# A two-layer attention and expert kernel: rotation of the keys one tile earlier, the maxima's scores ahead of the mix, and the routing product over 112 rows

## What is computed

```python
kv_r = kv_c * cos + rotate_half(kv_c) * sin
scores = q_r . k_r                      # per head, 56 tokens x 1500 rows
attn = softmax(scores)
ctx_c = attn . kv_r
out = merged value and output weights applied to ctx_c
# layer 0, after the attention
cw = weights of the 4 chosen of 16 experts, 0 for the others
moe = sum over e of cw[e] * down_e(silu(gate_e x) * (up_e x))  + shared expert
```

## Time and profile before

| what | value |
|---|---|
| median of 3 runs | 3447.54 us (3446.84 to 3452.19) |
| profiled execution, own time | 3445.47 us |
| its span, first to last instruction | 3443.7 us |
| mean granted TensorE clock | 0.918 of full speed |
| PE busy | 2980.6 us, 87% |
| DVE busy | 2033.7 us, 59% |
| POOL busy | 1769.7 us, 51% |
| ACT busy | 1261.3 us, 37% |
| DMA queues | 26.6% of 16 engines' span |

### The profile page before, as it was taken

How to read it: one execution, slowest core, us unless ns; L and a number is a source line. 1 busy time by engine, 2 the same in 40 slices (tenths; PEclk the granted TensorE clock), 3 DMA queues, 4 the chain that set the end, 5 groups by cost and what they waited for, 6 DMA issues and landing times. The chain is left out here.

```text
span 3443.7 us, 43529 instructions
## 1 busy us (share of the span) xinstructions
PE 2980.6 (87%) x16008; PEld 1691.6 (49%) x16008; DVE 2033.7 (59%) x2351; ACT 1261.3 (37%) x1747; POOL 1769.7 (51%) x1008
## 2 busy tenths in 40 slices
PE   7688978899888989888897789986997699888987
PEld 6444446444464444654445544453445444454445
DVE  3576656766467664676655556455645566446645
ACT  3124434244341444333443334332442244323432
POOL 0466723676436775366672247523771177315750
PEclk9789989899988999898998889988998899988998
DMA  7423213233114231132321233203321322122310
GB/s 253 118 61 87 62 40 92 72 81 81 34 60 110 63 84 50 61 101 57 74 58 50 88 77 76 74 6 86 78 52 51 86 60 67 53 61 67 83 56 6
DMA packets 117806, 247.54 MB, mean 72 GB/s; under 512 B 30415, under 2 KB 82879, under 8 KB 110038
## 3 DMA queue, kind: packets, MB, share of 16 engines
q1 hardware_dynamic: 117590, 244.57, 26.6%
HBM read 171.24 MB, written 48.27 MB: 64 GB/s over the span
## 5 line engine op out<-in xcount | busy, mean ns | idle before, releaser
L1215 POOL TENSOR_TENSOR sums<-sums,prob 125x896 f32<-125x896 f32 x528 | 1119.8, 2121 | 174.8 <-ACT prob L1102 125.0
L1331 DVE TENSOR_REDUCE maxpart<-pair 112x2 f32<-112x1000 f32 x720 | 861.5, 1197 | 464.1 <-PE pair L851 464.1
L1102 ACT ACTIVATE prob<-wide 125x896 f32<-125x896 f32 x768 | 704.3, 917 | 886.5 <-PE wide L877 884.5
L892 PE MATMUL single<-prob,kv 125*64 125x448 f32 x3072 | 758.1, 572 | 0.9
L872 PE MATMUL wide<-qhigh,kparts 64*125 64x448 f32 x3072 | 461.6, 378 | 0.0
L851 PE MATMUL pair<-kparts,qhigh 64*112 64x500 f32 x1440 | 358.3, 494 | 61.5 <-DVE maxpart L1331 47.3
L851 PEld LDWEIGHTS pair<-kparts,qhigh 64*112 64x112 f32 x1440 | 129.3, 176 | 489.8 <-DVE maxpart L1331 399.8
L1215 POOL TENSOR_TENSOR sums<-prob 125x896 f32<-125x896 f32 x64 | 134.4, 2100 | 408.4 <-ACT prob L1102 408.4
L872 PEld LDWEIGHTS wide<-qhigh,kparts 64*125 64x125 f32 x3072 | 283.3, 187 | 110.3 <-issue 81.2
L877 PE MATMUL wide<-shift,ones_row 64*125 64x448 f32 x1536 | 290.2, 373 | 48.8 <-DMA shift<-maxrow 48.8
L872 PE MATMUL wide<-qlow,kparts 64*125 64x448 f32 x1536 | 288.3, 370 | 0.0
(11 more groups left out here) (322 smaller groups left out, 4268.9 us busy)
## 6 DMA issues: line engine op xcount, KB each, us to landing
kparts<-keys_merged SPq DMA_DIRECT2D x64, 750.0 KB, 9.0
wexp_low_values<-in_experts SPq DMA_DIRECT2D x68, 384.0 KB, 3.1
kparts<-kparts SPq DMA_DIRECT2D x96, 250.0 KB, 3.1
keys_merged<-kparts SPq DMA_DIRECT2D x32, 750.0 KB, 7.6
recip<-zrec_merged SPq DMA_DIRECT2D x112, 112.0 KB, 2.8
raw<-in_ctx SPq DMA_DIRECT2D x33, 375.0 KB
w_low_values<-w_merged SPq DMA_DIRECT2D x64, 192.0 KB, 3.1
values_merged<-kv SPq DMA_DIRECT2D x32, 375.0 KB
```

What stands on the lines that cost most here:

```text
L892: mm = pe.matmul(mix_acc[64 * half:64 * half + DC, 0:HQ], kv[:, j % 3, t, :], prob[:, (j * LT + t) % NPROB, half * HQ:(half + 1) * HQ], st ...
L1102: nc.scalar.activation(prob[:, n_ % NPROB, :].rearrange("p (a b) -> p a b", a=2), acc[0:LP, :, 0:HQ], ACT.Exp)\
L1215: nc.gpsimd.tensor_tensor(dst, first_in, prob[:, n_ % NPROB, :], ALU.add).then_inc(s["pool_sum"], 1)
L1331: V.tensor_reduce(maxpart[:, j % 2, t:NMAX:4, b], acc[0:TQ, :, 0:LB], AX.X, ALU.max).then_inc(*R.signal_drained(kind, *key))
```

## The change

- A new constant `CWLOW = 96` takes the place of 32 for the low part of `cwT` and of `pick`. Both are then 112 rows high, with zeros in partitions 16 to 95, and the product `weight` goes over 112 rows.
- `rotate(j + 3)` stands at the start of the last tile of batch j, where `rotate(j + 2)` stood at the start of tile 0; only `rotate(2)` is at tile 0 of batch 0.
- `ropecos` is at tiles 0 and 1, `rope` at tiles 2 and 3.
- `stash` is at the last tile, was at tile 9.
- `maximum(*ahead)`, which adds `smax`, is put right after `score` (and `maxneg`), ahead of `mix`, in both layers.

```diff
-            if layer == 0 and t == 0 and j + 2 < BG:
-                add("rotate", j + 2)
+            if layer == 0 and t == 0 and j == 0:
+                add("rotate", 2)
+            if layer == 0 and t == LT - 1 and j + 3 < BG:
+                add("rotate", j + 3)
...
             add("score", j, t, region=t % 2)
             if j + 1 < BG and t == 8:
                 add("maxneg", j + 1)
+            if ahead[0] < BG:
+                maximum(*ahead)
             if last is not None:
                 add("mix", *last)
...
-            if layer == 0 and t == 9 and j + 2 < BG:
+            if layer == 0 and t == LT - 1 and j + 2 < BG:
                 add("stash", j + 2)
-            if ahead[0] < BG:
-                maximum(*ahead)
...
-            if layer == 0 and t in (1, 2) and j + 2 < BG:
-                add("ropecos", j + 2, t - 1)
-            if layer == 0 and t in (3, 4) and j + 2 < BG:
-                add("rope", j + 2, t - 3)
+            if layer == 0 and t in (0, 1) and j + 2 < BG:
+                add("ropecos", j + 2, t)
+            if layer == 0 and t in (2, 3) and j + 2 < BG:
+                add("rope", j + 2, t - 2)
...
-        cwT = buf("cwT", [32 + E0, NT], F32R)
+        cwT = buf("cwT", [CWLOW + E0, NT], F32R)
...
-                        pe.matmul(acc[:, 0:NT], c["pick"][:, i - 1:i].broadcast_to([32 + E0, 128]), cwT[:], start=True, stop=True)\
+                        pe.matmul(acc[:, 0:NT], c["pick"][:, i - 1:i].broadcast_to([CWLOW + E0, 128]), cwT[:], start=True, stop=True)\
...
-                        V.tensor_tensor(cwT[32:32 + E0, :], acc[0:E0, 0:NT], cwT[0:E0, :].bitcast(F32), ALU.subtract).then_inc(*R.signal_drained(kind))
+                        V.tensor_tensor(cwT[CWLOW:CWLOW + E0, :], acc[0:E0, 0:NT], cwT[0:E0, :].bitcast(F32), ALU.subtract).then_inc(*R.signal_drained(kind))
```

More of the change, by code:

```diff
@@ L35 @@
 MT = -(-HID // 128)
+CWLOW = 96
 ZP, ZC = 56, 8
@@ L305, in build_program @@
         bias0 = sb("bias0", [TR, E0])
-        pick = sb("pick", [32 + E0, E0], F32R)
+        pick = sb("pick", [CWLOW + E0, E0], F32R)
         ones_row = sb("ones_row", [128, LP + 1], F32R)
@@ L360, in _ @@
                 dve.wait_ge(load, 7 * 16)
-                for r in (0, 32):
+                for r in (0, CWLOW):
                     nc.vector.tensor_copy(pick[r:r + E0, :], ident[r:r + E0, r:r + E0])
```

## The result

The changed kernel takes 3472.54 us (median of 4 runs, 3465.21 to 3473.29), the one before 3447.53 us (4 runs): a ratio of 1.0065, 95% interval 1.0047 to 1.0082. It is slower, by 25 us by the medians and 16 to 28 by the interval, and lies above the range. The profiled execution after took 3473.29 us with a span of 3471.5, against 3445.47 and 3443.7.

| stage | before, us | after, us | difference |
|---|---|---|---|
| up to the first exponential of layer 0 | 213.4 | 211.1 | -2.3 |
| the four attention loops of layer 0 | 951.7 | 969.4 | +17.6 |
| experts and preparation, up to the loop of layer 1 | 846.5 | 836.1 | -10.4 |
| the four attention loops of layer 1 | 835.0 | 858.0 | +22.9 |
| the rest of layer 1 | 597.0 | 596.9 | 0.0 |

A forecast was written before the change was run, and what follows sets the result against it. PE's own work was taken to bound the loop, leaving its waits to win. -18.2 - 7.0 + 7.7 - 1.0 = -18.5 us from the profiled 3445.47 gave 3427.0, plus 2.1 for the median: 3429 us, range 3403 to 3448.

The forecast's parts named there:

- Part 1, routing: Experts of layer 0: 112-row product saves 0.41 us in 56 turns, less 4.8 us for late `hid_low`: -18.2 us.
- Part 2, the ropes: Layer 0: earlier `rope` removes the 1.15 us wait of the first key transposes, 24 times; DVE fills in tiles 0 to 4.
- Part 3, the stash: Last tiles of a batch: moving `stash` leaves SP's order of DMAs unchanged and gains nothing.
- Part 4, layer 0: Attention loops: 0.36 us at tile 8 goes, partly given back at tile 0; with the ropes -1.8 a group, -7.0 us.
- The chain: Layer 0: from raw-context load to the `score` waiting for `shift`, fixed at 9.56 us by the DMA queue, whatever PE does.
- the second wait: Layer 0, tile 0, batches 2 to 5: `smax` waits some 1.2 us for tile 11's reduction, delaying `mix` 0.9 us, 16 times.
- the -0.2 for batch 6: Layer 0, batch 5 to 6: no raw load, `smax` of tile 0 waits some 0.5 us; -0.2 us per group.
- The clock: Layer 0, tile 0, batches 2 to 5: low-clock stretches in all 16 windows at 1.25 us each: +7.7 us.
- the slow rival: Layer 0, tile 0: the double wait puts two low-clock stretches behind each of 16; clock +39.7, total 3461 us; chance 6%.
- Its bar in number: Slow rival's threshold in layer 0: some 9 of the 16 windows with two low-clock stretches, the rest with one.
- its bar in cost: Slow rival's threshold: it decides once the clock in layer 0 costs more than 26.2 us.
- Layer 1: Layer 1 loops: tile 8's reduction, `share` and `smax` start 0.9 us earlier, the 0.30 us wait nearly stays: -1.0 us.

The follow-up runs named there:

- the change with both waits taken away: The changed kernel with the raw load issued behind the copies into `shift` and `share` behind the reduction of tile 11: 3350.20 us, 0.9739; second run 3354.72 us, 0.9741.

## Why the prediction was wrong

**Part 1, routing: right in kind, and near in size.** -18.2 was forecast. The turn fell from 1.01 to 0.63 us, `hid_low` came late in some experts as forecast, and the part alone gave 20 us (14 to 26) by its ratio, 12.9 by its profile. In the experts themselves it is 14.8 us in 52 turns, where 52 x 0.41 = 21.3 would be the whole: what `hid_low` takes back there is 6.5 us, and 4.8 were put down for it.

**Part 2, the ropes: right**, the 1.15 us are gone. But the step took all of them for the ropes' own; `smax` ahead of `mix` takes them away too. This left the sum as it was, and hid how large the loss by part 4 is: alone the ropes win 38 us by the medians and 43 by the ratio, and with `smax` ahead nothing more (the full change, 1.0065, is what the two `smax` parts and the routing make without them: 1.0037 x 1.0084 x 0.9942 = 1.0063). DVE had more room than the step says, too. It put all four halves at 1.27 us, the mean of `rope`; after, `rope` takes 0.76 us and `ropecos` 0.66 on average, and DVE is busy for 20.05 us of a batch instead of 21.67. The shortest `rope` of either trace takes 0.55 us; the two before, of 1.33 us each, run beside POOL's additions (from 314.65 for 9.21 us, in the batch of the earlier trace rows).

**Part 3, the stash: never tried by itself;** nothing in the traces speaks against the forecast of nothing, and the run of the ropes, which moves it too, leaves nothing over for it.

**Part 4, layer 0: right.** Forecast were -7.0 us for the waits (-1.8 a group, which is -7.2). Measured: from the first exponential to the score of tile 8 of batch 0 a group is 0.7 to 1.2 us shorter, 3.9 in all; then the four windows of batch 1 119.1 to 113.1 us, the idle time of the 16 cycles 2.0 us less, the windows of batch 6 1.9 us longer; four groups together -3.9 - 6.0 - 2.0 + 1.9 = -10. The chain kept its length (9.50 to 10.09 us), and the second wait came where and as forecast. In place of the -0.2 for batch 6 stands +0.5 each, by the cause of layer 1.

**The clock: the first step that failed.** "I expect it in all 16, at 1.25 each": all 16 it was, but 12 of them with two stretches. PE's busy time in these windows is 496.6 us where 454.7 are needed (the change with both waits taken away), 41.9 us or 2.6 each; before it was 469.3 against 453.2, 16.1 us. So the term was +26, not +7.7. The wrong idea was that the second wait would soak up part of the slow stretch and cost nothing more.

The runs show what the second wait does. Three kernels have both waits (the change, `smax` ahead in layer 0 alone, and the one with POOL's addition narrowed in layer 1), 48 turns in all, and every one has a low stretch. In 36 turns it began between 0.84 us before and 0.53 us after the start of the matmul that had waited for `shift`, in nearly all of them ahead of the second wait, and all 36 were of double length. In the other 12 it began 2.37 to 2.92 us after that matmul, behind both waits, and was single. With the wait for `shift` alone (`share` later) 6 of 16 began that early and only 2 of them were double; one more began 1.60 us after. So the second wait goes with the doubling and with the late stretches. It can't have begun those that started ahead of it; why these came in 36 turns of 48, and in 6 of 16 without it, is open. The first wait was a little longer there (2.04 to 2.66 us against 1.99 to 2.49).

This is nearly the slow rival, which had a chance of 6%: it said two stretches behind each of the 16, and it was 12. Its bar in number (9 of 16) was passed; its bar in cost (26.2 us) was just missed by the 25.8 measured, since a doubled stretch cost 2.9 us and not 3.25. By the clock alone the change would have come out about even with the kernel before.

**Layer 1: the second step that failed.** "`share` starts a `mix` (0.9 us) earlier, and so does `smax` of tile 0; its 0.30 us stay": forecast -1.0, measured +22.9. The step moved the start of `share` and took its end along. The warning was there: `ctx_n` took 0.63 us in the earlier trace rows, while its group in the trace of before has a mean of 0.84 (median 0.63, longest 1.43), so elsewhere it took longer, and I did not look where. Its end in layer 1 hangs on POOL's addition, which did not move. The cost then is the one that I worked out for layer 0 and not for layer 1: a `mix` held up, 1.0 us, 20 times.

With both terms put right, -18.2 - 7.0 + 26 + 23 is +24 against the +25 of the medians. That it fits so well is in part luck: in the profiled executions the stage of the experts gained 10.4 us and not 18.2, and the loops of layer 0 lost 17.6 and not 19. No rival had the second term; the slow rival, 3461, had the first.

## What to carry to other kernels

A step moved ahead of another on an in-order engine takes over that one's slack: ask what the moved step waits for, in every loop that runs the same schedule, and take the end of that work from its releaser and from what runs beside it, not from its start plus a duration. When the mean of a group differs from the row in view, look at the longest members before the duration is used. And a small store that a wait hangs on goes ahead of a large load on the same queue: moving one issue of SP's won 36 us on the kernel before, by itself.

## What the runs showed of the hardware

- The same VectorE product of two SBUF tensors took 0.63 us alone and 1.43 and 2.27 in the rows shown beside an addition on GpSimd, and ended 0.48 us behind it in both kernels; a reduction out of PSUM kept its 1.20 us beside the same additions. Where a product on VectorE of 0.55 us went through in the middle of an addition, the addition took 3.06 us instead of 2.10.
- PE's two waits (2.35 and 0.81 us in the batch shown, 0.74 us apart) had the lower clock level begin in or behind them in all 16 cases. With a wait of 1.99 to 2.49 us and no second it was 7 of 16; with one of 1.36 to 2.15, and a second of at most 0.48, 3 to 10 of 16 (five kernels: before, routing, ropes, both together, and `smax` ahead in layer 1). Where PE did not wait for `shift` it was none or one of 16, and none behind the 20 waits of 1.06 to 1.18 us of layer 1.
- One stretch at the lower level cost 1.5 us of a batch and two 2.9 (1.5 and 3.25).
- A product over 48 rows among products over 128 cost 0.41 us beyond its own step (1.01 us for three steps); over 112 rows the three steps took 0.63.
- What waits for the store of the reciprocal to land was let through 1.95 us after its issue, and 5.64 us after it where the raw load had been issued half a microsecond ahead.
